# Normalisations of a two-layer decoder: each chunk's exponential directly behind its logarithm

## The reference

```python
x = layernorm(x + rwkv(x))              # its inner block has two affine layer norms, ln1 and ln2
x = layernorm(x + attention0(x, ctx))   # 1601 context tokens with a mask, 16 heads
x = layernorm(x + gated_ffn(x))
x = layernorm(x + recurrent_block(x))   # two RMS norms inside
x = layernorm(x + attention1(ctx, x))
x = layernorm(x + mixture_of_experts(x))  # 8 experts, the best 2 for each token

def layernorm(x):   # the version between blocks, no affine part
    m = mean(x, axis=-1); v = var(x, axis=-1)
    return (x - m) / sqrt(v + 1e-5)
def rms_norm(x, g):
    return x / max(norm(x), 1e-12) * 256 ** 0.5 * g
```

## Time and profile before

| | |
|---|---|
| median of 3 runs | 2132.68 us |
| lowest and highest of them | 2129.54 and 2134.18 us |
| the profiled execution | 2129.16 us |
| its span | 2127.2 us |
| mean granted TensorE clock, of full speed | 0.92 |
| PE busy | 1792.3 us (84%) |
| DVE busy | 1099.2 us (52%) |
| ACT busy | 948.7 us (45%) |
| POOL busy | 263.3 us (12%) |

### The profile page before, as it was taken

One profiled execution on the slowest core, in us unless ns is written; L12 is line 12 of the kernel. 1 busy time (PEld: TensorE's weight loads), 2 busy tenths in 40 slices (PEclk: granted clock), 3 DMA queues, 4 the chain that ended last, 5 costly groups with the idle time before them and its releaser, 6 DMA issues.

```text
span 2127.2 us, 45769 instructions
## 1 busy us (share of the span) xinstructions
PE 1792.3 (84%) x16832; PEld 930.0 (44%) x16833; DVE 1099.2 (52%) x1482; ACT 948.7 (45%) x1663; POOL 263.3 (12%) x215
## 2 busy tenths in 40 slices
PE   6879977999789875785999999999999709999980
PEld 2334423444334332231455545545553407777760
DVE  4653337877221240644888878878882412222225
ACT  3331234777521234331388868768789102222220
POOL 4134010000110100311000000000000150000005
PEclk9989997999899988796899999999999759999995
DMA  9101041110100000435000000000000720101013
GB/s 334 46 33 48 0 87 58 28 33 25 57 0 0 5 0 0 49 43 124 9 11 18 11 17 12 10 18 10 10 3 3 329 96 28 35 30 35 30 32 111
DMA packets 64171, 97.14 MB, mean 46 GB/s; under 512 B 11504, under 2 KB 56752, under 8 KB 62074
## 3 DMA queue, kind: packets, MB, share of 16 engines
q1 hardware_dynamic: 60922, 86.21, 14.2%
q0 software_dynamic: 3072, 8.39, 1.2%
HBM read 65.20 MB, written 28.97 MB: 44 GB/s over the span
## 4 chain that ended last, share of the span: by engine, by line
PE 56%; DVE 5%; issue 4%; POOL 4%; ACT 2%; DMA 1%; SPq 0%; DVEq 0%; ACTq 0%; POOLq 0%
PE ps L517 9%; PE ps L1118 9%; PE ps L1813 9%; PE ps L1186 8%; PE ps L1161 8%; PE ps L1827 5%; PE ps L1469 2%; DVE arena L1321 2%; PE ps L441 1%; PE ps L1223 1%; POOL rows_in L1921 1%; POOL arena L1926 1%; PE ps L1821 1%; DMA qparts<-arena 1%; PE ps L1171 1%
## 5 line engine op out<-in xcount | busy, mean ns | idle before, releaser
L1270 ACT ACTIVATE arena<-ps 128x512 f32<-128x512 f32 x1088 | 598.1, 602 | 173.1 <-PE ps L1186 139.6
L1321 DVE TENSOR_REDUCE arena<-ps 128x1 f32<-128x802 f32 (+1 forms) x512 | 494.1, 989 | 73.4 <-PE ps L1118 71.5
L517 PE MATMUL ps<-arena 128*128 (+1 forms) x832 | 382.1, 620 | 73.4 <-DVE arena L1610 23.2
L1118 PE MATMUL ps<-arena 97*32 97x400 bf16 (+2 forms) x5120 | 357.6, 356 | 52.8 <-DVE arena L1321 23.8
L1186 PE MATMUL ps<-arena 100*32 100x512 bf16 x4352 | 388.5, 385 | 9.9 <-issue 5.8
L1161 PE MATMUL ps<-arena 128*32 128x256 f32 x4352 | 333.9, 381 | 1.5 <-ACT arena L1270 0.9
L517 PEld LDWEIGHTS ps<-arena 128*128 128x128 f32 x832 | 163.8, 199 | 290.6 <-issue 290.6
L1118 PEld LDWEIGHTS ps<-arena 97*32 97x32 bf16 x5120 | 129.9, 97 | 209.6 <-DVE arena L1321 70.4
L1813 PE MATMUL ps<-arena 128*128 x608 | 193.7, 461 | 0.8 <-ACT arena L1880 0.8
L1161 PEld LDWEIGHTS ps<-arena 128*32 128x32 f32 x4352 | 135.4, 111 | 100.7 <-issue 8.7
L1186 PEld LDWEIGHTS ps<-arena 100*32 100x32 bf16 x4352 | 120.4, 97 | 132.0 <-ACT arena L1270 34.0
(11 more groups left out here) (188 smaller groups left out, 1418.4 us busy)
## 6 DMA issues: line engine op xcount, KB each, us to landing
arena<-in_experts_w SPq DMA_DIRECT2D x8, 2176.0 KB, 17.4
arena<-qparts SPq DMA_DIRECT2D x192, 64.0 KB, 2.3
qparts<-arena SPq DMA_DIRECT2D x48, 128.0 KB, 2.0
rows_in<-arena SPq DMA_DIRECT2D x1, 5120.0 KB, 34.8
arena<-in_ctxT SPq DMA_DIRECT2D x3, 1664.0 KB, 9.1
kparts<-arena SPq DMA_DIRECT2D x24, 208.0 KB, 2.4
arena<-kparts SPq DMA_DIRECT2D x12, 416.0 KB, 14.3
arena<-rows_in SPq DMA_DIRECT2D x38, 128.0 KB, 2.0
```

The source lines that it names most:

```text
L517: ins = eng.matmul(out, w[:, k, m * P:(m + 1) * P], x[:, k, tok(c)], start=k == 0, stop=k == ktiles - 1)
L1118: ins = eng.matmul(slot_banks(s_static)[j:j + 32, x, 0:n_keys], Qst[0:97, ring, heads[x], q * P + j:q * P + j + 32], Kst[0:97, at_head(rin ...
L1270: eng.activation(probs[:, keys_of(u, kt) % 2, h, :], ring_bank(r), ACT.Exp, bias=0.0).then_inc(ring_read.sem, 1)
L1321: eng.tensor_reduce(MX[:, par, heads[0] * QT + q, n % 2:n % 2 + 1], got, AX.XY, ALU.max).then_inc(slot_free.sem, 1)
```

## The change

In ScalarE's part of `normalise` the loop of four logarithms and the loop of four exponentials become one loop, written out, in which the exponential of a chunk follows its logarithm. The exponential waited for all four logarithms once; it now waits for the logarithm of its own chunk, four times.

```diff
                 with eng.Fori(0, NC) as c:
                     centred.wait(eng, c) if centre else ready(eng, c)
                     eng.activation(SQ[:, :, tok(c)], body[:, :, tok(c)], ACT.Square).then_inc(squared.sem, 1)
-                with eng.Fori(0, NC) as c:
+                for c in range(NC):
                     if centre:
                         var.wait(eng, c)
                         eng.activation(norm_rstd[:, tok(c)], bank(c).squeeze(1), ACT.Ln,
...
 
                         eng.activation(norm_rstd[:, tok(c)], norm_rstd[:, tok(c)], ACT.Ln, bias=0.0,
                                        scale=RMS_SCALE).then_inc(logged.sem, 1)
-                logged.wait_all(eng)
-                with eng.Fori(0, NC) as c:
+                    logged.wait(eng, c)
                     eng.activation(norm_rstd[:, tok(c)], norm_rstd[:, tok(c)], ACT.Exp,
                                    bias=0.0 if centre else UNSCALE, scale=-0.5).then_inc(rstd.sem, 1)
```

## The result

The changed kernel takes 2113.05 us (median of 4 runs, 2112.10 to 2115.03); the kernel before took 2131.11 beside it (4 runs, 2128.34 to 2134.18). The ratio is 0.9915, 95% interval 0.9900 to 0.9931: faster by 18.1 us, with 14.7 to 21.3 as its bounds. The profiled execution took 2113.43 us with a span of 2111.3, 15.9 less than the span before.

A forecast was written before the change was run, and what follows sets the result against it. TensorE held 56% of the chain of waits; what counted was how early VectorE's scaling begins. Gains 3.0+1.8+2.7+1.7+0.1+0.9 = 10.2 us took the median 2132.7 to 2122.5 us; 8-in-10 range 2115.5 to 2129.5.

The forecast's parts named there:

- The mechanism: All nine normalisations: earlier exponentials let VectorE's scaling begin earlier, a gain only where later work waits for it; 10.2 us.
- covers named for norm1, rms2 and norm3: Weight cast in norm1, GpSimd adds in rms2, key and context loads after norm3 hide earlier scaling: gains 0, 0.1, 0.
- rms1's product: rms1: scaling starts right after VectorE's fourth clip, so TensorE's product starts at 761.9 instead of 763.69, a gain of 1.8.
- Rival (d): Activation tables are reloaded at each alternation of logarithm and exponential: about 34 us slower, 2167; chance 0.03.
- Rival (a): Only the last scaling counts: norm2 and norm4 keep 3.0+2.7, norm0 and rms1 bring nothing; 2127.0 us; chance 0.20.
- (c): Lock, DMA and key copies also cover norm0 and rms1, and the dear pair price holds: 3.5 us, 2129.2; chance 0.04.
- The step that failed: norm0: the last logarithm frees the banks, the product starts at about 292.5, and later stores and loads move along; gain 1.7.
- rival (b): TensorE's clock doesn't fall at the products of norm0 (1.6 more) and rms1 (2.3 more): 14.1 us, 2118.6; chance 0.11.
- The pair: ScalarE's price for a logarithm with its exponential, 0.81+0.53 = 1.34 us, or 1.63 at the dear end.
- norm4: Pairs set the pace; the last scaling ends at 1674.43 against 1677.12, and the router's products wait for it: gain 2.7.
- norm2: The last scaling ends at 745.82 instead of 748.80, and everything behind waits for it: gain 3.0.
- ln2's 0.9: After ln2: GpSimd's work moves some 3 us earlier, changing phase with the eight squares; between -0.7 and +1.9, taken as 0.9.

The follow-up runs named there:

- e3: The new order in norm2, rms1 and norm4 alone, against the kernel before: 2121.9 us, ratio 0.9956.
- e4: The new order in norm0 alone, against the kernel before: 2124.97 us, ratio 0.9975.
- e5: The new order in rms2 alone, against the kernel before: 2132.37 us, ratio 0.9997.
- e6: The new order in ln1, ln2, norm1 and norm3 alone, against the kernel before: 2131.24 us, ratio 0.9996.
- e7: The changed kernel with GpSimd's cast of the FFN weights moved from norm1 to ahead of norm0: 2107.59 us, ratio 0.9886 to the kernel before.
- e8: The changed kernel with GpSimd's four adds for the saved sum held back behind rms2's scaling: 2109.63 us, ratio 0.9894 to the kernel before.
- e1: The kernel before with both loops written out, order of logarithms and exponentials as before: 2132.09 us, ratio 1.0006.
- e12: The changed kernel with the cast ahead of norm0, the adds behind rms2's scaling and no rms1 table load: 2103.2 us, ratio 0.9855 to the kernel before.
- e11: The changed kernel without rms1's activation table load: 2111.37 us, ratio 0.9898 to the kernel before.

## Why the prediction was wrong

**What was right.** The mechanism, and where it pays. Only the stages where nothing else ends later gain: e3 and e4 carry it, e5 and e6 show nothing clear of zero. The covers named for norm1, rms2 and norm3 are the ones that hold: lifting two of them (e7, e8) brings their gains out, and norm3's store takes up the earlier start (18.33 us instead of 13.06). rms1's product was forecast 1.8 sooner behind its fourth clip and is 2.0 sooner. Rival (d), table reloads, is refuted by the timelines (its five terms add up to 37 us, not 34). Rival (a), that norm0's earlier first chunk brings nothing, is refuted by e4; so is (c).

**The step that failed** is norm0's: "the product starts at about 292.5, a gain of 1.7. What follows is a line of stores and loads on SP that begins with the first query part, at 301.48, so it moves along." It moved by more than that. The change in this stage alone is worth 5.3 us (3.4 to 7.2). The trace of e4 gives 1.6 for the product's start, which the step had, and 1.6 more because the 32 products no longer begin at 1.2 GHz. That was known, as rival (b), with the right size for norm0 (1.6), but it got a chance of 0.11 instead of a place in the sum. The argument against it, that other stages fall after idling no longer, weighed a comparison between stages above the one row that mattered: the clock fell in the very microsecond of the start. For rms1 the sum puts the clock at nothing in the same way: 0.7 of that rival's 2.3 came behind the product, whose clock is still low from 754.0 to 757.4 (before from 761.7 to 768.5), and another 1.6 came later in the recurrent block (e3). That the two make 2.3 together is luck, since the rival had it all at the product.

**Mis-sized terms.** The pair was priced 0.60+0.21+0.53 = 1.34 us and measured 1.15. The 0.21 came from the only place where the trace of before has an exponential behind a logarithm, the entry into a new loop; e1 shows 0.03 for the same wait in written-out code. Over three pairs and the last exponential that is 0.6 to 0.75 us in each stage where pairs set the pace: norm4 3.3 instead of 2.7, norm2 3.4 instead of 3.0. ln2's 0.9 didn't show: the product behind its squares stands 1.4 us later in the trace after, a lag that begins in ln1's variances, ahead of anything that the change touches, where the clock stayed low longer; e6 has ln1, ln2, norm1 and norm3 together at 0.9 us (-1.7 to 3.4), so 0.9 for ln2 is neither shown nor refuted by the times.

**The range.** Its low end, 2115.5, took the clock's gain as the far end of a rival and cut it off. With the clock's terms and the measured pair price the sum is 3.4+2.0+0.7+1.6+3.3 for e3's stages and 2.4+1.6 for norm0: 15.0.

**What stays open.** Of the 18.1 us some 3 are not put down to a step. About 2 of e4's lie behind the first query store and have no place yet. In rms2 the trace after has 2.1+0.5 us that e5 doesn't have; the traces of e3 and e5 show how two parts of the change can be worth more together there, but no run has only those two. Why the clock falls where it does stays open too: in rms1, behind the same 2.47 us of idle time, it fell in the changed kernel, e3, e8 and e12 and held in e7 and e11. Single runs of e1, with the order unchanged, lie between 2123.3 and 2140.1, so shifts of a few us come by themselves.

## What to carry to other kernels

When a wait of TensorE ahead of a stage gets shorter, look at the granted clock in the first microseconds of that stage: where it fell there, the gain can be the wait and what the lower clock cost the products behind it (all of it in norm0, 0.7 of 2.3 us in rms1), and this belongs into the sum. Take the price of a dependent step from a place where the code has the same form; here the step into a second engine-run loop cost 0.21 us, the wait in written-out code 0.03. Where an earlier result stands behind a blocking transfer, cast or sum on another engine, that cover is the next thing to move: here two covers and a spared table load were worth 12.8 us beside the change's 18.1.

## What was not expected of the hardware

- In written-out code a ScalarE operation that waits for the one before it through a semaphore starts 0.03 us behind its end; the next, independent one starts some 0.09 us before its predecessor's end (289.76+0.63 against 290.30).
- When two-input VectorE operations meet GpSimd's on SBUF, both sides pay: four scalings 8.57 us instead of 4.84, the cast beside them 5.04 instead of 4.03 where it runs apart.
- Loading a table set that is already there isn't skipped: 1.28 us at L484, and 1.0 of it on the path in e11.
